# Attention softmax sums: all nine full text tiles added up off TensorE, and the maxima, reciprocals and projections placed anew

## The reference, cut to what matters

```python
q = rms_norm(linear(x, q_w, q_b), norm_q_w).reshape(B, L, NH, HD)
img_x = attention(q, k_img, v_img)      # softmax over 257 image keys
txt_x = attention(q, k, v)              # softmax over 1344 text keys
return linear((txt_x + img_x).reshape(B, L, DIM), o_w, o_b)
# around it: x = x + tanh(g) * xattn(layernorm(x), ctx), then x = x + tanh(g) * moe_ffn(layernorm(x))
```

## Time and profile before

| what | value |
|---|---|
| median of 3 | 1834.37 us (1830.43 to 1834.69) |
| profiled execution | 1831.94 us, span 1830.7 us, clock 0.993 |
| PE busy | 1764.8 us (96%) |
| PE weight loads busy | 1113.7 us (61%) |
| DVE busy | 1181.2 us (65%) |
| ACT busy | 824.2 us (45%) |
| POOL busy | 904.4 us (49%) |

### The profile page before, as it was taken

One profiled execution on the slowest core, in us unless ns is written; L12 is line 12 of the kernel. 1 busy time (PEld: TensorE's weight loads), 2 busy tenths in 40 slices (PEclk: granted clock), 3 DMA queues, 4 the chain that ended last, 5 costly groups with the idle time before them and its releaser, 6 DMA issues. The chain is left out here.

```text
span 1830.7 us, 25272 instructions
## 1 busy us (share of the span) xinstructions
PE 1764.8 (96%) x9078; PEld 1113.7 (61%) x9078; DVE 1181.2 (65%) x2276; ACT 824.2 (45%) x1516; POOL 904.4 (49%) x335
## 2 busy tenths in 40 slices
PE   5999999999999999999999999998899999999999
PEld 4888878874444444444444445433576787888777
DVE  5776686677787767787677786745554445443465
ACT  4443323345555545555455564564221165555221
POOL 3222312116776654776456674665143376776552
PEclk9999999999999999999999999999999999999999
DMA  9556749446444553444453443401231467888432
GB/s 311 153 169 193 233 157 246 162 150 157 117 121 107 135 136 77 111 126 108 124 136 90 105 122 93 119 13 70 62 127 58 161 208 262 276 267 252 145 121 93
DMA packets 185253, 268.77 MB, mean 147 GB/s; under 512 B 24972, under 2 KB 122012, under 8 KB 184612
## 3 DMA queue, kind: packets, MB, share of 16 engines
q1 hardware_dynamic: 180008, 250.36, 47.0%
q0 software_dynamic: 5120, 16.78, 2.7%
HBM read 194.10 MB, written 105.93 MB: 164 GB/s over the span
## 5 line engine op out<-in xcount | busy, mean ns | idle before, releaser
L631 DVE TENSOR_REDUCE mp<-ps 128x1 f32<-128x512 f32 (+2 forms) x1024 | 531.1, 569 | 182.8 <-PE ps L434 177.5
L1092 ACT ACTIVATE P<-ps 128x512 f32<-128x512 f32 (+1 forms) x832 | 447.8, 597 | 333.5 <-PE ps L959 323.0
L1260 POOL TENSOR_TENSOR sacc<-sacc,P 128x2048 f32<-128x2048 f32 x80 | 368.3, 4603 | 74.9 <-ACT P L1092 66.6
L434 PE MATMUL ps<-Kst,Qst 96*128 96x512 f32 (+2 forms) x1024 | 383.8, 384 | 6.5 <-DVE mp L631 5.8
L434 PEld LDWEIGHTS ps<-Kst,Qst 96*128 96x128 f32 x1024 | 191.8, 188 | 259.9 <-DVE mp L631 211.9
L959 PE MATMUL ps<-Qst,Kst 100*128 100x512 f32 (+1 forms) x832 | 322.3, 408 | 9.7 <-ACT P L1092 9.7
L914 PE MATMUL ps<-P,Vg 128*32 128x512 f32 (+2 forms) x1792 | 238.3, 606 | 0.0
L803 POOL TENSOR_TENSOR cl<-craw,ch 128x1024 fp32r<-128x1024 f32 (+2 forms) x26 | 62.0, 2384 | 285.3 <-ACT ch L539 285.3
L959 PEld LDWEIGHTS ps<-Qst,Kst 100*128 100x128 f32 (+1 forms) x832 | 150.9, 186 | 76.9 <-ACT P L1092 35.0
L49 PE MATMUL ps<-W,ch 128*128 128x512 f32 (+1 forms) x408 | 162.4, 398 | 0.0
L51 PE MATMUL ps<-W,cl 128*128 128x512 f32 (+1 forms) x408 | 160.1, 393 | 0.0
(11 more groups left out here) (230 smaller groups left out, 2999.2 us busy)
## 6 DMA issues: line engine op xcount, KB each, us to landing
gur<-in_w_gate_up SPq DMA_DIRECT2D x23, 1024.0 KB, 7.8
Kst<-KHd SPq DMA_DIRECT2D x32, 640.0 KB, 8.0
Vd<-vf SPq DMA_DIRECT2D x50, 256.0 KB, 2.3
craw<-in_ctxT SPq DMA_DIRECT2D x24, 512.0 KB, 4.4
KHd<-sth SPq DMA_DIRECT2D x24, 512.0 KB, 3.5
KLd<-stl SPq DMA_DIRECT2D x24, 512.0 KB, 4.7
dnr<-in_w_down SPq DMA_DIRECT2D x23, 512.0 KB, 3.9
xg<-Xg SPq DMA_DIRECT2D x23, 512.0 KB, 8.0
```

Of the source, the lines that this page charges most:

```text
L434: pe.matmul(ps[:, bank, 0:c1 - c0], Qst[G % 3][0:96, j, 128 * qt:128 * qt + 128], Kst[G % 2][0:96, j, c0:c1], start=True, stop=True).then_ ...
L631: dve.reduce_max(mp[:, 4 * qt + j, c:c + 1], ps[:, bank, 0:c1 - c0], AX.X).then_inc(d_ra, 1)
L1092: act.activation(P[slot(G, kt)][:m, j, :], ps[:m, 2 + (e - 1) % 3, :], ACT.Exp, scale=SCALE).then_inc(a_exp, 1)
L1260: pool.tensor_tensor(sacc[:], x[:], P[slot(G, kt)][:], ALU.add).then_inc(g_sum, 1)
```

## The change

- Tiles 3 and 5 lose their totals on PE. POOL adds tiles 0 and 1 (at step 2), DVE adds tile 2 into `sacc` (at step 3, between the fifth unit and the sixth), and POOL adds tiles 3 to 8, one in each of the steps 4 to 9. The chain passes from POOL to DVE and back by `g_sum` and `d_add`.
- The totals that stay follow their weightings without other matmuls between: tiles 9 and 10 (text) at step 11; tile 10 (image) weighed and `sacc` totalled at step 12; tile 11 weighed, tiles 10 and 11 totalled at step 0, behind two units; tile 12 at step 1. ACT's two copies of the text banks part: bank 6 at step 11, bank 7 at step 12.
- The three text parts of the maxima are 448, 448 and 448 keys instead of 512, 512 and 320.
- The reciprocals move from step 11 to steps 5 to 8, one in each. The projected tiles move from steps 1 and 2 to the ends of steps 4, 6, 8 and 10.
- POOL's `image_total` moves behind the first `add` of its group, to step 2.

```diff
-    CH = [(0, 512), (512, 1024), (1024, NTXT), (NTXT, NKP)]
+    CH = [(0, 448), (448, 896), (896, NTXT), (NTXT, NKP)]
...
+        def text_end(G):
+            weigh(G, 9, 0, 128, False, False)
+            weigh(G, 10, 0, 64, False, True)
+            pe.wait_ge(a_si, G) if G else pe.wait_ge(d_ones, 1)
+            total(G, 9, 0, 128, True, False)
+            total(G, 10, 0, 64, False, False)
+
+        def text_total_and_image(G):
+            weigh(G, 10, 64, 128, True, False)
+            pe.wait_ge(g_sum, 7 * G + 7)
+            pe_heads(7, lambda j: ones[:, :], sacc, 0, 128, False, True).then_inc(p_tot, 1)
...
+            scored(0)
+            place(0)
+            scored(1)
+            place(1)
+            if kt == 1 and G:
+                image_end(G - 1)
+            if 3 <= kt < 11:
+                weigh(G, kt - 2, 0, 128, False, False)
+            if kt == 11:
+                text_end(G)
+            if kt == 12 and more:
+                pe.wait_ge(d_mn, 4 * (G + 2))
+                pe_mrow(ra_bank())
+                ra += 1
+            place(2)
+            scored(2)
+            place(3)
+            scored(3)
+            place(4)
+            place(5)
+            if kt == 2:
+                weigh(G, 0, 0, 128, True, False)
+            if kt == 12:
+                text_total_and_image(G)
...
-                if fk in (3, 5, 9, 10, 11, 12):
+                if fk == 2:
+                    act.wait_ge(d_add, fG + 1)
+                elif fk < 9:
+                    act.wait_ge(g_sum, sum_no(fG, fk))
+                else:
                     act.wait_ge(p_tot, tot_no(fG, fk))
...
+            if kt == 3 and G < NG:
+                dve.wait_ge(a_exp, exp_no(G, 2, 3))
+                dve.wait_ge(g_sum, sum_no(G, 1))
+                dve.tensor_tensor(sacc[:], sacc[:], P[slot(G, 2)][:], ALU.add).then_inc(d_add, 1)
+            units(G + 1, upto[5], sum(plan[5:]))
+            if 5 <= kt < 9 and 1 <= G < NG:
+                if kt == 5:
+                    dve.wait_ge(g_oi, 4 * pG + 2)
+                cs = slice(128 * (kt - 5), 128 * (kt - 5) + 128)
+                dve.reciprocal(rt2[:, pG % 2, cs], rt2[:, pG % 2, cs]).then_inc(d_inv, 1)
...
+            if kt == 3:
+                pool.wait_ge(d_add, G + 1)
+            pool.tensor_tensor(sacc[:], (P[slot(G, 0)] if kt == 1 else sacc)[:], P[slot(G, kt)][:], ALU.add).then_inc(g_sum, 1)
...
-            if G < NG and kt - 1 in ON_POOL:
+            if G < NG and kt == 2:
+                add(G, 1)
+            if kt == 2 and 1 <= G < NG:
+                image_total(G - 1)
+            if G < NG and 4 <= kt < 10:
                 add(G, kt - 1)
-            if kt == 1 and 1 <= G < NG:
-                image_total(G - 1)
```

More of the change, by code:

```diff
@@ L108, in program @@
     d_mx, d_mn = sem("d_mx"), sem("d_mn")
+    d_add = sem("d_add")
     p_sc, a_exp = sem("p_sc"), sem("a_exp")
@@ L976, in total, with image, image_end @@
         def total(G, kt, p0, p1_, first, last):
[L977 to L983, removed]
-            pe_heads(7, lambda j: ones[p0:p1_, :], P[slot(G, kt)], p0, p1_, first, last).then_inc(p_tot, 1)
+            pe_heads(7, lambda j: ones[p0:p1_, :], P[slot(G, kt)], p0, p1_, first, last).then_inc(p_tot, 1)
+        def text_end(G):
[8 more added lines that the diff above has]
+            pe_heads(7, lambda j: ones[:, :], sacc, 0, 128, False, True).then_inc(p_tot, 1)
+        def image(G):
+            weigh(G, 11, 0, 128, False, False)
+            pe.wait_ge(a_txt, 2 * G + 2)
+            total(G, 10, 64, 128, True, False)
+            total(G, 11, 0, 128, False, False)
+        def image_end(G):
+            weigh(G, 12, 0, 65, False, True)
+            total(G, 12, 0, 65, False, True)
         for step in range(NSTEP):
             G, kt = divmod(step, NKT)
-            pG, pk = divmod(step - 2, NKT)
-            late = step >= 2 and pk in (0, 10)
             more = G + 1 < NG
@@ L996, in place, with scored @@
                 units(G + 1, upto[i], plan[i])
[L998 to L1019, removed]
+            def scored(j):
+                if G < NG:
+                    score(G, kt, j)
@@ L1021, in pe_attend @@
             if kt == 0:
-                weighing()
                 place(0)
-                totalling()
                 place(1)
+                if G:
+                    image(G - 1)
                 place(2)
                 for j in range(4):
-                    if G < NG:
-                        score(G, kt, j)
+                    scored(j)
                     place(3 + j)
[L1031 to L1065, removed]
+                continue
+            scored(0)
+            place(0)
@@ new lines, in pe_attend @@
+            place(5)
[3 more added lines that the diff above has]
+                text_total_and_image(G)
+            place(6)
+            if G in (5, 9, 13) and kt in (4, 6, 8, 10):
+                if kt == 4:
+                    pe.wait_ge(a_ath, G - 1)
+                    pe.wait_ge(g_atl, G - 1)
+                    if G == 5:
+                        pe.wait_ge(g_wol, 2)
+                pe_project_tile((kt - 4) // 2, ra_bank())
+                ra += 1
@@ L1183, in dve_attend @@
             upto = [at + sum(plan[:i]) for i in range(8)]
-            units(G + 1, at, sum(plan[:2]))
             if step == 2:
@@ L1198, in dve_attend @@
                 dve.tensor_tensor(oi[:], ps[:, 6, :], rt2[:, pG % 2, :], ALU.mult).then_inc(d_oi, 1)
[L1199 to L1209 removed]
+            if kt == 3 and G < NG:
[8 more added lines that the diff above has]
+                dve.reciprocal(rt2[:, pG % 2, cs], rt2[:, pG % 2, cs]).then_inc(d_inv, 1)
+            if G in (5, 9, 13) and kt in (4, 6, 8, 10):
+                dve_project_tile((G - 5) // 4, (kt - 4) // 2, ra, BANKS_RA[(ra - 65) % 3])
+                ra += 1
             for i in range(3):
```

47 lines of the change are left out of this document (16 added, 31 removed).

## The result

The changed kernel takes **1909.3 us** in the median of four runs (1893.56 to 1917.47); the kernel before, beside it, 1832.72. The ratio is 1.041 (95% interval 1.033 to 1.049). Against the 1834.37 us from which the forecast was made, it is slower by 75 us where 16 were forecast, and it lies 41 us above the range. The profiled execution took 1901.77 us, with a span of 1900.5.

The account below looks back on a forecast made before the run. POOL's chain behind DVE's add, through the wait for the maxima, was to replace PE as bound. Middle groups +7, projected groups -3, group 0 +3, last group +10: +17 on 1834.4, taken as 1850 us; range 1828 to 1868.

Parts of the forecast that it names:

- PE's clock: Rival: last group's idle stretch had clock 0.93; a longer half-clock wait could add 2 or 3 us; no separate chance.
- groups with projected tiles: Groups 5, 9 and 13: projected tiles cover POOL's chain and the reciprocals; 63.0 against 64.1 us, -1.1 each.
- PE's way from the maxima row to DVE's add: Middle group's opening: 2.85 to the total of `sacc`, step 0 5.2, step 1 2.9, to step 3 5.9, add's end 6.2.
- DVE's add: Step 3, tile 2, 2048 elements on 128 partitions: taken as 2.3 us, with unit loads waiting for it.
- The shift: Negated maxima on DVE wait for POOL's add 8 and first normalising instruction: 1.6 us behind `sacc`, bounds 0.5 and 2.9.
- the shift is dearer: Rival: both normalising instructions get ahead and DVE's add meets `image_total`, 2.6 us in 11 groups: 1879 us; chance 0.09.
- six adds: POOL adds tiles 3 to 8 in a row behind DVE's add, 4.68 us each: 28.1 us.
- step 4: Its third unit waits for a bank freed behind DVE's add: 5.3 us instead of 3.4, 1.9 lost.
- the row of ten units at steps 1 and 2: Merged cluster leaves ten units in a row, DVE 5.9 us against PE's 3.5: 1.2 us lost.
- The reciprocals: Moved between units of steps 5 to 8, 0.85 us each on DVE: 0.3 us a step, 1 us of PE's chain.
- The last group: No units, so POOL's chain is bare: +10.7 us less 1 that PE saves behind it, +10.
- relief of PE: Rival: PE's saved 2.8 us a group come through, limit 1805 us, or 1823 with half the stalls; chance 0.14.

Follow-up runs that it names:

- e2: Changed kernel with six unused 512-column matmuls ahead of the wait for the maxima in each of the first 15 groups: 1.0304 of the kernel before.
- e3: Changed kernel with only the sums put back (totals of tiles 3 and 5 on PE, no add on DVE): 1.0119 of the kernel before.
- e9: Changed kernel with the old sums and the image total of tile 12 back behind the last score of step 1: 1.0060 of the kernel before.
- e4: Kernel before with only the text parts of the maxima made 448, 448 and 448 keys: 1.0002 of the kernel before.
- e5: Changed kernel with the old sums and the reciprocals back in step 11: 1.0106 of the kernel before.
- e6: Kernel before with the changed sums alone; places of totals, reciprocals, projections and parts stay: 1.0215 of the kernel before.
- e7: Kernel before with thirty chained small memsets on DVE ahead of the negated maxima in groups 1 to 14: 1.0179 of the kernel before.
- e16: Kernel before with tile 3 also added on POOL (one total less on PE) and chained memsets ahead of the negated maxima: 1.0147 of the kernel before.
- e15: e12 with the totals' matmuls of steps 5 and 7 issued on PE again, their result unused: 1.0537 of the kernel before.
- e17: Kernel before with the changed sums and the three equal parts of 448 columns: 1.0239 of the kernel before.
- e18: e12 with the old parts of 512, 512 and 320 columns: 1.0330 of the kernel before.
- e1: Changed kernel with the transposes of the maxima moved behind the total over `sacc`: 1.0384 of the kernel before.
- e12: Changed kernel with late transposes of the maxima and the image total of tile 12 behind step 1's last score: 1.0347 of the kernel before.
- e13: e12 with DVE's one add cut into four quarters spread among the units: 1.0398 of the kernel before.

## Why the prediction was wrong

**The step that failed** is the rival "PE's clock": "the last group's idle stretch had 0.93; a longer wait at half clock could add 2 or 3 us. Within the range." It looked for the clock only in the last group and put nothing for the others. The prediction itself puts waits of PE into the middle groups, and nine of those eleven groups met half clock. Free of it the changed kernel's middle group takes 54.2 to 54.8 us; the mean is 56.8. So about 2.3 us x 11 = 25 us are clock, and another 25 are the schedule, of which the prediction had 7. The three groups with projected tiles lost some 9 us more to the clock, by an estimate: 68.1 us against about 65.0, which is e2's 66.4 less its six added matmuls (1.4 us; in these groups no wait hides them). e2 bears this out: 25 us back with the middle groups at full clock. The clock alone doesn't account for the whole miss, for e2 with its 1884.7 us is still 17 above the range; the rest is in the two paragraphs on sizes and on projected tiles below.

**Sized too small: PE's way from the maxima row to DVE's add.** The walk gave 52.85 us for a middle group, and about 54.5 is what it takes undisturbed. In the group from 749.32 to 804.07 the stages were, with the prediction's figure behind each: transposes to total of `sacc` 3.5 (2.85), step 0 5.5 (5.2), step 1 with its cluster 3.1 (2.9), on to step 3 6.4 (5.9), to the end of DVE's add 6.4 (6.2), the adds 28.3 with the gap before them (28.1), the shift 1.6 (1.7). No single term is it: 1.8 us are missing ahead of the end of DVE's add, 0.33 of them a score's wait for ACT. In the other undisturbed group, from 451.92 on, it is 1.3.

**The shift** came out as sized, by another way. The prediction let a scalar_tensor_tensor wait for the first normalising instruction, 1.6 us behind `sacc` in all. It was the tensor_scalar in front of it that took 1.30 us beside that instruction (802.51), and the scalar_tensor_tensor then took 0.17 and ended 1.5 us behind `sacc`. That a tensor_scalar isn't held, which the prediction took from the 0.17 us of the earlier trace rows, was right for the first one (797.92, beside an add) and wrong for the second. The Trainium skill ("SBUF — State Buffer", Who interferes with whom) says that tensor_scalar can take both ports; the row of 1.30 us agrees. The 14 us that the prediction worked out by that rule did not come: the second normalising instruction started together with the last scalar_tensor_tensor (803.85 and 803.84) and didn't get ahead. So it went at ten of the eleven middle groups; at the last (the row at 1281.11) both tensor_scalars were held, 1.21 and 1.25 us. DVE's add didn't meet `image_total` either, which ended 1.6 us before it (826.40 and 1.27 us, the add at 829.27), so the rival "the shift is dearer" fell.

**Right, in its size:** DVE's add, 2.28 us (2.3 said); six adds 28.20 us (28.1) that begin behind it; step 4, 5.4 us (5.3), with PE's wait of 1.27 us in it; the row of ten units at steps 1 and 2, 7.22 us against 6.16 (1.2 said), shown by e3 and e9; equal parts at nothing (e4). The reciprocals, priced at 1 us of PE's own chain, cost nothing to speak of (e3 against e5). The last group lost about 8 us (10 said), and in it `sacc` came 7.9 us later behind the maxima row, so POOL's chain holds there. The first lost 5.2 with the start (3 said), but some 3 us of half clock lie in it, so that number is in part luck. In both kernels with the sums, relief of PE comes to nothing, as said.

**Wrong, and open in part of its cause:** groups with projected tiles were to win 1.1 us each. They lost 4.0, about 3 of it to the clock, and so still lose about 1 where it is whole. POOL's chain is covered in them, as the prediction said: the maxima rows wait for PE (4.76 us idle of DVE ahead of 749.96), so it is PE's own way that is longer than the 63.0 us said. PE stands in them as in the others, 0.66 us at step 2 (699.22) and 1.27 at step 4 (709.27), ahead of the first projected tile. The moved tiles with the old sums and tile 12 put back take 64.2 us (e9), the sums with the tiles in their old places 65.2 to 65.9 (e6): the loss comes with the sums. Why nothing of the two totals saved is left stays open. The 5.9 us that the part behind attention won is not explained either.

**What opens the half clock** is settled only in part. Shown: a wait of 1.2 us at step 12 doesn't open it by itself (e7, e16). It isn't decided by the load of the totals at steps 5 and 7 (e15), by one total less (e16), by the parts (e17, e18) or by the wait for the maxima (e1, e12). Matmuls put ahead of that wait end it in the middle groups but for the last (e2). In the profiled executions it goes with the changed sums, and with them and the changed order it comes in nearly every group: six and eight stretches with the sums in the old order (e6, e17), 14 in the new one (e12, e18), two and none with the new order and the old sums (e3, e9; but other executions of e9 had a lower clock). Not shown: that the order does this by what stands around a wait. The same row of instructions fell at 810.50 in e6 and didn't at 864.20, so something outside the order also decides, perhaps the moment at which the wait comes. The versions differ in the length of their groups, and so in these moments, and no run changes the one without the other. Whether the clock stays up with no stall at all in the changed order was not reached either: e13 only moved the stall.

## What to carry to other kernels

Where TensorE is the bound, price a new wait not only by its length: ask what the clock could do after it, in every group and not only where it is low already, and look in the profile for the same matmul in two lengths (here 1.06 and 1.93 us). Taking work off the bounding engine paid in a small step, as long as its helper opened no wait: one total less brought the last maxima row 6.9 us forward, about half a microsecond a group, while two totals less with the new order cost 4.6 us a group. Leave the work where the engine would idle anyway: in the last group the freed microsecond cost 11 in the profiled execution.

## What the runs showed of the hardware

- Added work can shorten a kernel: six unused matmuls in each of 15 groups gave 25 us (e2), at a granted clock of 0.985 instead of 0.970 in the profiled executions.
- A wait of 1.20 us in each group, followed by one of about 1.0, left the clock at 1.00 (e7); two groups with the same instructions and the same wait of 1.25 us differed in it (e6).
- A tensor_scalar of 128x16 took 0.17 us beside one POOL instruction and 1.30 us beside another; what decides it no run took apart. The 1.30 us came back at ten of the eleven middle groups, each time with 0.17 or 0.18 us for the scalar_tensor_tensor behind it.
